# Attention inner loop on TensorE: score and value matmuls issued by two pairs of key blocks instead of one

## The reference, cut to what matters

```
x = x + attn(layernorm(x))            # 32 x 2048 x 1024
x = x + ffn(layernorm(x))

def attn(x):                          # 16 heads of 64, causal
    q, k, v = split(x @ W_qkv.T)
    q, k = rope(q), rope(k)
    scores = q @ k.T / sqrt(64);  scores[key > query] = -inf
    return (softmax(scores) @ v) @ W_o.T
```

## Time and profile before

| | |
|---|---|
| median of 3 runs | 6319.74 us |
| the profiled execution: time of its slowest core | 6333.9 us |
| its span in the trace (core 3) | 6332.0 us |
| spans of the 8 cores | 6290.3 to 6332.0 us |
| busy: TensorE matmul, VectorE, ScalarE, GpSimd | 4398.2, 2246.0, 1703.3, 1415.3 us |

### The profile page before, as it was taken

How to read it: one execution, slowest core, us unless ns; L and a number is a source line. 1 busy time by engine, 2 the same in 40 slices (tenths; PEclk the granted TensorE clock), 3 DMA queues, 4 the chain that set the end, 5 groups by cost and what they waited for, 6 DMA issues and landing times. The chain is left out here.

```text
span 6332.0 us, 47366 instructions; the slowest of 8 cores (6290.3 to 6332.0 us)
## 1 busy us (share of the span) xinstructions
PE 4398.2 (69%) x11412; PEld 1063.9 (17%) x11412; DVE 2246.0 (35%) x2561; ACT 1703.3 (27%) x1983; POOL 1415.3 (22%) x1736
## 2 busy tenths in 40 slices
PE   0166888885346788888336788888634678888843
PEld 0022111112112111112012211111201221111211
DVE  1244333334434333333434433333343433333244
ACT  0000444440000244442000044444000024444300
POOL 0027000002326400000341800000133550000023
PEclk9989555557569655556558755555656975555565
DMA  5410000002021000002021000000202100000101
GB/s 138 115 44 17 1 0 1 1 4 67 20 103 27 7 1 1 0 1 68 2 93 45 19 1 1 1 1 1 70 10 104 34 11 0 1 1 1 45 25 63
DMA packets 151776, 180.51 MB, mean 29 GB/s; under 512 B 89951, under 2 KB 110559, under 8 KB 151015
## 3 DMA queue, kind: packets, MB, share of 16 engines
q1 hardware_dynamic: 151532, 177.48, 9.1%
HBM read 133.41 MB, written 44.04 MB: 28 GB/s over the span
## 5 line engine op out<-in xcount | busy, mean ns | idle before, releaser
L613 ACT ACTIVATE PT<-pss,ecol_s 128x1024 bf16<-128x1024 f32 x1280 | 1427.7, 1116 | 2470.9 <-PE pss L595 2466.8
L560 DVE RECIPROCAL rb<-po 64x512 f32<-64x512 f32 x256 | 859.9, 3359 | 2230.7 <-PE po L550 2230.7
L595 PE MATMUL pss<-qkT 64*128 64x512 bf16 x2560 | 1316.2, 616 | 0.0
L528 PE MATMUL po<-PT,v 128*65 128x512 bf16 (+3 forms) x2560 | 1224.9, 565 | 34.6 <-POOL PT L628 33.1
L628 POOL TENSOR_SCALAR_AFFINE_SELECT PT<-PT 128x128 bf16<-128x128 bf16 x1024 | 275.0, 292 | 2970.1 <-ACT PT L613 2969.5
L550 PE MATMUL po<-lr,ones_s 1*64 1x512 f32 x512 | 494.8, 1067 | 380.6 <-ACT lr L543 380.6
L462 PE MATMUL psq<-u1T,wqk 128*128 128x512 bf16 x2048 | 510.6, 396 | 194.3 <-DVE t1b L475 194.3
L852 PE MATMUL psz<-t,ones_s 128*1 128x512 f32 x256 | 225.3, 1034 | 367.9 <-DVE t L841 367.9
L528 PEld LDWEIGHTS po<-PT,v 128*65 128x65 bf16 x2560 | 274.3, 140 | 1189.8 <-issue 1166.5
L488 POOL TENSOR_TENSOR t2b<-qks,ropeB_s 128x512 f32<-128x512 f32 x256 | 324.8, 1269 | 650.9 <-DVE t1b L475 614.7
L353 PE MATMUL ptr<-ident_s,u1b 128*128 128x128 bf16 x512 | 49.7, 255 | 589.8 <-DVE u1b L338 589.8
(11 more groups left out here) (94 smaller groups left out, 2128.4 us busy)
## 6 DMA issues: line engine op xcount, KB each, us to landing
xb<-x SPq DMA_DIRECT2D x64, 512.0 KB, 4.0
xr<-x SPq DMA_DIRECT2D x64, 512.0 KB, 4.2
out<-x2o SPq DMA_DIRECT2D x64, 512.0 KB, 2.6
wqk<-wqk_b SPq DMA_DIRECT2D x64, 256.0 KB, 3.0
cbuf_f<-wqk SPq DMA_DIRECT2D x16, 512.0 KB, 4.8
wvb<-wv_b SPq DMA_DIRECT2D x32, 256.0 KB
wob<-wo_b SPq DMA_DIRECT2D x32, 256.0 KB
wqk_b<-cbuf_b SPq DMA_DIRECT2D x16, 256.0 KB, 2.8
```

The lines of the kernel that those rows point to most:

```text
L528: e.matmul(pso[i_hqb % 2][0:65, sigma:512], vsb[:, j * NH * 66 + h * 66: j * NH * 66 + h * 66 + 65], PT[:, sl4 * 512 + sigma: sl4 * 512 + ...
L560: e.reciprocal(rb[sl][:, :], posb[sl][64:128, :])
L595: e.matmul(pss[sl2][:, (jj % 2) * 512: (jj % 2) * 512 + 512], qkT[hb:hb + 64, kcol + jj * 128: kcol + (jj + 1) * 128], qkT[hb:hb + 64, qco ...
L613: e.activation(PT[:, slot0 * 512: slot0 * 512 + 1024], pss[sl2][:, :], AF.Exp, bias=self.ecol[:, 1:2], scale=0.125) \
```

## The change

The loop over pairs becomes a loop over groups of two pairs. For a group it adds both score pairs (one to each `pss` buffer), then both value pairs of the group before with their tail if there is one, and then both exps with their masks. `K // 2` is always even, so a group never spans two query blocks. No instruction is added or taken away, no buffer is changed, and what each instruction waits for is worked out by the same rules.

```diff
-                    for pl in range(K // 2):
-                        j0, j1 = 2 * pl, 2 * pl + 1
...
-                        self.add("tensor", _smm)
...
-                        self.add("scalar", _exp)
...
-                                self.add("gpsimd", _msk)
-                        if pending is not None:
-                            ph, pqb, pi, pK, pexp, pmsk, pjs = pending
-                            plan_pv(ph, pqb, pi, pK, pexp, pmsk, pjs)
-                            if pjs[-1] == pK - 1:
-                                plan_tail(ph, pqb, pi)
-                        pending = (h, qb, i_hqb, K, exp_done, msk_done, [j0, j1])
+                    for pl0 in range(0, K // 2, 2):
+                        group = []
+                        for pl in (pl0, pl0 + 1):
+                            j0, j1 = 2 * pl, 2 * pl + 1
...
+                            self.add("tensor", _smm)
+                            self.s_smm.inc(2)
+                            group.append((pl, j0, j1, sl2, self.s_smm.n))
+
                         if pending is not None:
+                            for (ph, pqb, pi, pK, pexp, pmsk, pjs) in pending:
+                                plan_pv(ph, pqb, pi, pK, pexp, pmsk, pjs)
+                                if pjs[-1] == pK - 1:
+                                    plan_tail(ph, pqb, pi)
+
+                        newpend = []
+                        for (pl, j0, j1, sl2, w_smm) in group:
+                            slot0 = j0 % 4
+                            w_pt = max(self.pt_free[slot0],
+                                       self.pt_free[slot0 + 1])
...
+                            self.add("scalar", _exp)
+                            v_exp = self.s_exp.inc()
+                            self.pss_free[sl2] = v_exp
+                            exp_done[pl] = v_exp
...
+                            newpend.append((h, qb, i_hqb, K, exp_done,
+                                            msk_done, [j0, j1]))
+                        pending = newpend
```

More of the change, by code:

```diff
@@ L573, in p2a @@
                     msk_done = {}
-                    for pl in range(K // 2):
-                        j0, j1 = 2 * pl, 2 * pl + 1
[L576 to L602, removed]
-                        self.add("tensor", _smm)
[L604 to L616, removed]
-                        self.add("scalar", _exp)
[L618 to L634, removed]
-                                self.add("gpsimd", _msk)
-                                msk_done[j] = self.s_msk.inc()
-                        if pending is not None:
-                            ph, pqb, pi, pK, pexp, pmsk, pjs = pending
-                            plan_pv(ph, pqb, pi, pK, pexp, pmsk, pjs)
-                            if pjs[-1] == pK - 1:
-                                plan_tail(ph, pqb, pi)
-                        pending = (h, qb, i_hqb, K, exp_done, msk_done, [j0, j1])
@@ new lines, in p2a, with _smm, _exp, _msk @@
+                    for pl0 in range(0, K // 2, 2):
+                        group = []
+                        for pl in (pl0, pl0 + 1):
+                            j0, j1 = 2 * pl, 2 * pl + 1
+                            gp = self.gpair
+                            self.gpair += 1
+                            sl2 = gp % 2
+                            w_free = self.pss_free[sl2]
+                            qcol = (2 * (h // 2)) * S
+                            kcol = (2 * (h // 2) + 1) * S
+                            hb = 64 * (h % 2)
+                            w_head = (self.qkT_base + (2 * (h // 2) + 2) * NQB
+                                      if (qb == 0 and pl == 0) else 0)
+                            def _smm(e, qb=qb, j0=j0, sl2=sl2, wf=w_free,
+                                     qcol=qcol, kcol=kcol, hb=hb, wh=w_head):
+                                if wh:
+                                    e.wait_ge(self.s_qkT.h, wh)
+                                if wf:
+                                    e.wait_ge(self.s_exp.h, wf)
+                                for jj in (j0, j0 + 1):
+                                    e.matmul(pss[sl2][:, (jj % 2) * 512:
+                                                      (jj % 2) * 512 + 512],
+                                             qkT[hb:hb + 64, kcol + jj * 128:
+                                                 kcol + (jj + 1) * 128],
+                                             qkT[hb:hb + 64, qcol + qb * 512:
+                                                 qcol + qb * 512 + 512],
+                                             start=True, stop=True) \
+                                     .then_inc(self.s_smm.h, 1)
+                            self.add("tensor", _smm)
+                            self.s_smm.inc(2)
+                            group.append((pl, j0, j1, sl2, self.s_smm.n))
+                        if pending is not None:
+                            for (ph, pqb, pi, pK, pexp, pmsk, pjs) in pending:
[7 more added lines that the diff above has]
+                                       self.pt_free[slot0 + 1])
+                            def _exp(e, sl2=sl2, slot0=slot0, w=w_smm, wp=w_pt):
+                                e.wait_ge(self.s_smm.h, w)
+                                if wp:
+                                    e.wait_ge(self.s_pvmm.h, wp)
+                                e.activation(PT[:, slot0 * 512:
+                                                slot0 * 512 + 1024],
+                                             pss[sl2][:, :], AF.Exp,
+                                             bias=self.ecol[:, 1:2],
+                                             scale=0.125) \
+                                 .then_inc(self.s_exp.h, 1)
+                            self.add("scalar", _exp)
+                            v_exp = self.s_exp.inc()
+                            self.pss_free[sl2] = v_exp
+                            exp_done[pl] = v_exp
+                            for j in (j0, j1):
+                                if j >= 4 * qb:
+                                    sigma = (j - 4 * qb) * 128
+                                    col = (j % 4) * 512 + sigma
+                                    def _msk(e, col=col, w=v_exp):
+                                        e.wait_ge(self.s_exp.h, w)
+                                        e.affine_select(
+                                            PT[:, col:col + 128],
+                                            PT[:, col:col + 128],
+                                            pattern=[[1, 128]],
+                                            compare_op=ALU.is_ge, fill=0.0,
+                                            base=0, channel_multiplier=-1) \
+                                         .then_inc(self.s_msk.h, 1)
+                                    self.add("gpsimd", _msk)
+                                    msk_done[j] = self.s_msk.inc()
+                            newpend.append((h, qb, i_hqb, K, exp_done,
+                                            msk_done, [j0, j1]))
+                        pending = newpend
```

## The result

| | before | after |
|---|---|---|
| median | 6320.88 us (beside the experiments, 13 runs each: 6318.83 and 6320.07) | 6238.75 us (6226.66 to 6269.67, 10 runs) |
| ratio to before | | 0.9879, 95% interval 0.9859 to 0.9899 |
| profiled execution, span | 6333.9, 6332.0 us | 6228.7, 6226.8 us |

The change makes the kernel 1.2% faster: 76 us by the ratio (64 to 89), where 60 were forecast. The time lies within the stated range. The profiled executions differ by more, 105 us, since the one before lay 13 us over its median and the one after 10 us under; some 20 us of these 105 lie outside the attention, where no instruction was changed.

The account below looks back on a forecast made before the run. TensorE, at 1.2 GHz, was taken to set attention's pace. Steps without a tail +200, with a tail -251, edges -11: -62 us on 6333.9, so 6272, or 6260 on the runs' median scale; range 6225 to 6350.

Parts of the forecast that it names:

- The ring: Attention steps without a tail: value pair, two exps, second score pair wait in a circle for `PT` slots; 4.43 us against 3.91.
- The overlapped exps: ScalarE, in the ring: two exps back to back take 2.12 us, or 2.25 if they do not overlap.
- the wake-up of TensorE by an exp: In the ring: end of exp to a score matmul, taken as 0.18 us, downward 0.12, upward 0.25.
- value pair to exp: In the ring: from the first value pair's start to the exp waiting for its slots, 1.17 us.
- The steps without a tail: 384 attention groups not followed by a tail: each 0.52 us longer, +200 us in all.
- The step with a tail: 256 attention groups followed by a tail: 5.88 us in place of 6.86, -251 us in all.
- The edges: Start and end of each attention stage: about -2.7 us a stage, -11 us in all.
- The first tail: At a stage's start: fp32 matmul 2.21 us after the first value pair in place of 3.91.
- The 1 us at a stage's end: Last value pairs of a stage follow each other without scores between, some 1 us sooner.
- The ring did not win: Rival 1, steps without a tail: longer ring outweighs the tails' gain, 6342 us or up to 6401; chance 0.16.
- The turns: Rival 3, TensorE between scores and values: ring hidden, 640 groups save 0.25 us each, -160 us, 6160; chance 0.04.
- The clock: Rival 4, TensorE in attention: clock rises to 2.4 GHz, some 810 us less, 5510; chance 0.03.

Follow-up runs that it names:

- experiment 2: The changed kernel with eight `PT` slots in place of four, used in turn by pairs: 5976.68 us, ratio 0.9441 to the kernel before.
- 4: The kernel before the change with eight `PT` slots in place of four, as a control: 6316.23 us, ratio 0.9988.
- 7: The changed kernel, four slots, with the copy behind the next group's exps and the fp32 matmul behind its score pairs: 6303.03 us, ratio 0.9976 to before.
- experiment 1: The kernel before the change, with only ScalarE's copy of the sums moved ahead of the next query block's exp: 6187.68 us, ratio 0.9774.
- Experiment 3: The changed kernel with the copy of the sums put back behind the next group's first exp: 6438.55 us, ratio 1.0193 to the kernel before.
- the same late tail: The changed kernel with copy behind the next group's exps, fp32 matmul behind its score pairs: 5714.18 us with eight slots, 6303.03 us with four.

## Why the prediction was right, point by point

- **The ring.** Shown by the trace after and by experiments 2, 4 and 7. Its size was off by 0.07: 4.43 forecast, 4.36 measured, the low end of the bounds. The overlapped exps were 2.12, also with two waits each. The other three terms were each a little too large: the wake-up of TensorE by an exp, taken as 0.18, was 0.14 to the score matmul (2244.18 to 2244.32); from there to the value pair it was 0.94 and not 0.96; and value pair to exp was 1.16 and not 1.17. No row stood behind the 0.12 that gave the low bound, so that the sum met this bound exactly is luck. The steps without a tail cost 173 us and not 200, which by itself puts the sum at -89.
- **The step with a tail.** 5.88 forecast and measured. Its parts: experiment 1 gives 0.59 for the copy no longer behind an exp; the other 0.39, by the rows and by no experiment, are a turn each way (0.25), the copy's start no longer paced by masks (0.09), and, for the small rest, a value pair that no longer waits for its masks ahead of its start. Experiment 3 takes the copy's place away again and loses more than the whole gain.
- **The edges.** The first tail gave its 1.7 us per stage, but the prediction counted its saving twice, here and among the 256 steps with a tail, which makes 4 us. The 1 us at a stage's end is there in the changed kernel (1.02), but the kernel before had 0.58 of it already, which the prediction overlooked; 0.4 is the gain.
- **The rivals.** The ring did not win, since the exps do overlap. The turns are real: with the ring open a score group and the value group behind it are 1.82 apart (2286.46 to 2288.28, experiment 2) and back 1.85, for 1.71 of columns, so 0.11 and 0.14 as in the earlier trace rows; but the change cashes them only at tails, so the drain that the Trainium skill ("TensorEngine Tiling (Array Packing)", Key Properties) names decides little here. No run shows that a drain is what a turn costs: in the trace the first weights after a turn also load only as their matmul starts (both at 2317.43), so a weight load that nothing hides is as good a reading. The clock stayed at its lower level.
- **Sum.** -62 forecast for the profiled execution; -83 by its steps and its copies, -76 (64 to 89) by the ratio. The ring's 27 us are most of the miss, and the two slips at the edges, some 6 us, take a little off it. Two terms of opposite sign, each two to three times the result, make a forecast of this kind fragile: with 0.2 us more in the ring the time would have been as before.

## What to carry to other kernels

Grouping work on one engine deepens the pipeline, and it needs buffers to match: two pairs in flight and two pairs' worth of `PT` slots closed a ring that cost 173 us. A `PT` twice as large gave 262 back: the 173, and some 90 of turns (3.91 - 3.67 = 0.24 for each of 384 steps) that the ring had swallowed. Before crediting a reordering to what it was built for, list what else it moved on each queue: here 0.59 of the 0.98 us that a tail gained, 151 of 251 us, came from one copy that stepped ahead of one exp. And take a wait off the path only after asking what stands behind it, for the same late tail won 262 us or lost 64, by the slots alone.

## What the runs showed of the hardware that was not expected

Two exps back to back overlap by 0.10 us even when each has two waits (2.12 for two of 1.11), while an exp and a copy behind it do not (2276.18 + 1.11 to 2277.32 in experiment 3, 0.03 between). And TensorE stayed at its 1.2 GHz level through attention in the windows above, though score and value matmuls fill 21 to 22 of 25 us; what holds it there no run here tried to find.
